# Turning x1 for the gated feed-forward network: from DMA blocks and a VectorE transpose to TensorE transposes

## The reference, cut to what matters

```python
x = L0_attn_x                                        # (2, 2048, 256)
x = layernorm(x + (h + m))                           # h = x + mamba2(rmsnorm(x)),  m = relu(rmsnorm(h) @ w_fc)**2 @ w_proj
def ffn(x):                                          # hidden width 1024, four layers of scaled ternary weights
    h = silu(tlin(x, w1, s1)) * tlin(x, w2, s2)      # 256 -> 1024, twice
    h = gelu(tlin(h, h1, sh1))                       # 1024 -> 1024
    h = gelu(tlin(h, h2, sh2))                       # 1024 -> 1024
    return tlin(h, w3, s3)                           # 1024 -> 256
out = layernorm(x + ffn(x))
```

## Time and profile before

| | |
|---|---|
| median of 3 runs | 1225.31 us (1225.02 to 1226.35) |
| the profiled execution | 1225.02 us |
| its span, first to last instruction | 1223.3 us |
| mean granted clock of TensorE | 0.997 of 2.4 GHz |
| busy: TensorE, VectorE, ScalarE, GpSimd | 98%, 64%, 53%, 19% of the span |

### The profile page before, as it was taken

How to read it: one execution, slowest core, us unless ns; L and a number is a source line. 1 busy time by engine, 2 the same in 40 slices (tenths; PEclk the granted TensorE clock), 3 DMA queues, 4 the chain that set the end, 5 groups by cost and what they waited for, 6 DMA issues and landing times.

```text
span 1223.3 us, 19219 instructions
## 1 busy us (share of the span) xinstructions
PE 1196.2 (98%) x6468; PEld 1007.0 (82%) x6468; DVE 783.2 (64%) x1363; ACT 646.0 (53%) x1213; POOL 232.8 (19%) x210
## 2 busy tenths in 40 slices
PE   8899999999999999999999999999999999999996
PEld 6678888888888888788888888888888888888885
DVE  6898898989899898855535336345363363543633
ACT  6788888878788888666224124142141331422420
POOL 0517153534434261610000000000000000000000
PEclk9999999999999999999999999999999999999998
DMA  7222211222322221134500202002002020020000
GB/s 268 97 82 75 83 68 51 63 88 75 97 75 97 75 73 64 66 128 182 201 1 1 52 1 51 0 0 51 0 6 45 0 51 0 0 51 0 18 1 18
DMA packets 60696, 72.05 MB, mean 59 GB/s; under 512 B 33520, under 2 KB 52080, under 8 KB 58736
## 3 DMA queue, kind: packets, MB, share of 16 engines
q1 hardware_dynamic: 60656, 71.51, 18.0%
HBM read 63.10 MB, written 22.03 MB: 70 GB/s over the span
## 4 chain that ended last, share of the span: by engine, by line
issue 53%; POOL 0%; DVE 0%; POOLq 0%; DVEq 0%
POOL rsv_b L1882 0%; DVE o_sb L1959 0%; POOLq L1880 0%; DVEq L1712 0%; POOL rsv L235 0%; POOLq L441 0%
## 5 line engine op out<-in xcount | busy, mean ns | idle before, releaser
L1866 ACT ACTIVATE full<-bank,scale 128x512 f32<-128x512 f32 x128 | 88.3, 690 | 383.0 <-PE bank L1774 383.0
L1774 PE MATMUL bank<-hB_hi,h_sb 128*128 128x512 f32 x512 | 199.6, 390 | 0.0
L1774 PE MATMUL bank<-hB_lo,h_sb 128*128 128x512 f32 x512 | 199.5, 390 | 0.0
L1774 PE MATMUL bank<-hA_hi,h_sb 128*128 128x512 f32 x512 | 199.3, 389 | 0.0
L1774 PE MATMUL bank<-hA_lo,h_sb 128*128 128x512 f32 x512 | 199.2, 389 | 0.0
L1928 DVE CAST hA_hi<-full 128x512 fp32r<-128x512 f32 x64 | 27.3, 427 | 173.1 <-ACT full L1866 173.1
L1882 POOL TENSOR_TENSOR rsv_b<-mv_b,eps 128x4 f32<-128x4 f32 x8 | 10.7, 1341 | 618.2 <-DVE mv_b L187 618.2
L1774 PEld LDWEIGHTS bank<-hA_hi,h_sb 128*128 128x128 f32 x512 | 96.1, 188 | 20.1
L1774 PEld LDWEIGHTS bank<-hA_lo,h_sb 128*128 128x128 f32 x512 | 96.1, 188 | 20.0
L1774 PEld LDWEIGHTS bank<-hB_hi,h_sb 128*128 128x128 f32 x512 | 96.3, 188 | 19.2
L1774 PEld LDWEIGHTS bank<-hB_lo,h_sb 128*128 128x128 f32 x512 | 96.3, 188 | 19.0
(11 more groups left out here) (230 smaller groups left out, 2981.5 us busy)
## 6 DMA issues: line engine op xcount, KB each, us to landing
chk_xh<-w_ffn SPq DMA_DIRECT2D x16, 704.0 KB, 4.2
ffn_raw<-w_ffn SPq DMA_DIRECT2D x8, 1408.0 KB, 6.7
h_sb<-ffn_raw SPq DMA_DIRECT2D x2, 4096.0 KB, 19.5
xT<-x_t SPq DMA_DIRECT2D x8, 512.0 KB, 6.2
x_res<-x SPq DMA_DIRECT2D x8, 512.0 KB, 3.8
x_rows<-x SPq DMA_DIRECT2D x8, 512.0 KB, 3.3
x_in<-x_rows SPq DMA_DIRECT2D x8, 512.0 KB, 4.9
x_in<-x SPq DMA_DIRECT2D x7, 512.0 KB, 4.9
```

Of the source, the lines that this page charges most:

```text
L1774: ins = pe.matmul(o, a_, b_, start=first and n == 0, stop=last and n == 1, skip_group_check=True)
L1866: nc.scalar.activation(full[:, n % FULL, :], b[:], ACT.Gelu, scale=scale[:, 1 + n // KH, n % KH:n % KH + 1]).then_inc(s_gd, 1)
```

## The change

Seven of the eight tiles were turned by DMA and VectorE. All are now turned as the first one was. `load_blocks`, its semaphore and the VectorE transpose are gone; in layer 2, ahead of channel 6, TensorE runs `turn(pe, i + 1)`; ScalarE and VectorE call `turned_hi` and `turned_lo`, which read PSUM where they read SBUF before. One number in a wait of VectorE (L1898) follows, since `s_ti` now counts ten a tile. The load of `x_in` is as it was.

```diff
@@ -1673,10 +1673,6 @@
         w3_sb = sb("w3_sb", [P, KH, D], F32R)
         s3_b = sb("s3_b", [P, D])
         x1_in, x1_res = x_in, sb("x1_res", [P, CH, D])
-        SQ = 32
-        BLOCK_LOADS = 16 * KD * (P // SQ)
-        x1_blocks = x1[:].rearrange("p c n -> p (c n)").rearrange("p (k n) -> p k n", k=KD)
-        x1T = chk_xh[:, PART:].rearrange("p (k n) -> p k n", k=KD)
         hA_hi, hA_lo = sb("hA_hi", [P, KH, TILE], F32R), sb("hA_lo", [P, KH, TILE], F32R)
         hB_hi, hB_lo = sb("hB_hi", [P, KH, TILE], F32R), sb("hB_lo", [P, KH, TILE], F32R)
         FULL = 3
@@ -1695,8 +1691,6 @@
         s_h2 = sem("h2_loaded")
         s_w3 = sem("w3_loaded")
         s_kept = sem("x1_kept")
-        s_blocks = sem("x1_blocks_loaded")
-        s_turned = sem("x1_blocks_turned")
         s_gi = sem("ffn_act_item_ready")
         s_shi = sem("hidden_hi_ready")
         s_ghi = sem("gated_hi_ready")
@@ -1715,15 +1709,6 @@
                 def load(at):
                     sp.dma_start(x1_in[:], rows(x1_dram, at)).then_inc(s_x1i, 16)

-                def load_blocks(at):
-
-                    flat = x1_dram.rearrange("n f -> (n f)")[bass.ds(at, TILE * D)]
-                    src = flat.rearrange("(m b k j a) -> j b k m a", b=SQ, k=KD, j=P // SQ, a=SQ)
-                    for j in range(P // SQ):
-                        for k in range(KD):
-                            dst = x1_blocks[j * SQ:(j + 1) * SQ, k, :].rearrange("b (m a) -> b m a", a=SQ)
-                            sp.dma_start(dst, src[j][:, k, :, :]).then_inc(s_blocks, 16)
-
                 def store(i, at):
                     sp.wait_ge(s_o, CH * i + CH)
                     sp.dma_start(rows(out, at), o_sb[:]).then_inc(s_store, 16)
@@ -1738,14 +1723,11 @@
                 sp.wait_ge(s_td, KD + B_DVE_BANKS)
                 sp.wait_ge(s_x1o, 16 * TILES + 1)
                 load(TILE * D)
-                load_blocks(TILE * D)
                 with sp.Fori(0, TILES - 2) as i:
                     at, at_next = sp.snap(i * (TILE * D)), sp.snap((i + 2) * (TILE * D))
                     store(i, at)
                     sp.wait_ge(s_kept, i + 2)
                     load(at_next)
-                    sp.wait_ge(s_turned, i + 1)
-                    load_blocks(at_next)
                 store(TILES - 2, (TILES - 2) * TILE * D)
                 i = TILES - 1
                 for n in range(2):
@@ -1811,6 +1793,8 @@
                         pe.wait_ge(s_h2, 16)
                         pe.wait_ge(s_w3, 16)
                     for j in range(KH):
+                        if more and j == TURN:
+                            turn(pe, i + 1)
                         channel(2, h2_sb, hB_hi, hB_lo, j)
                         if j >= BEHIND:
                             out_rows(j - BEHIND)
@@ -1866,9 +1850,7 @@
                         nc.scalar.activation(full[:, n % FULL, :], b[:], ACT.Gelu,
                                              scale=scale[:, 1 + n // KH, n % KH:n % KH + 1]).then_inc(s_gd, 1)
                         if more and n == 2 * KH + TURN - 1:
-                            act.wait_ge(s_turned, i + 1)
-                            for k in range(KD):
-                                nc.scalar.activation(x1T_hi[:, k, :], x1T[:, k, :], ACT.Copy).then_inc(s_thi, 1)
+                            turned_hi(act, i + 1)

                 with act.Fori(0, TILES - 1) as i:
                     tile(i, True)
@@ -1895,7 +1877,7 @@
                         nc.vector.tensor_tensor(lo, full[:, n % FULL, :], hi.bitcast(F32), ALU.subtract).then_inc(s_split, 1)

                     def gated(j):
-                        dve.wait_ge(s_ti, KH * i + KD + j + 1)
+                        dve.wait_ge(s_ti, NBD * i + KD + j + 1)
                         dve.wait_ge(s_gd, NBA * i + j + 1 + B_ACT_BANKS)
                         if j >= FULL:
                             dve.wait_ge(s_split, 3 * KH * i + j - FULL + 1)
@@ -1928,15 +1910,8 @@
                         nc.vector.tensor_copy(hi[:, n % KH, :], full[:, n % FULL, :]).then_inc(s_shi, 1)
                         dve.wait_ge(s_shi, 2 * KH * i + n - KH + 1)
                         lo(n, hi[:, n % KH, :], lo_[:, n % KH, :])
-                        if more and n == 2 * KH + TURN - 2:
-                            dve.wait_ge(s_blocks, BLOCK_LOADS * (i + 1))
-                            nc.vector.transpose(x1T.rearrange("p k n -> p (k n)"),
-                                                x1_blocks.rearrange("p k n -> p (k n)")).then_inc(s_turned, 1)
                         if more and n == 2 * KH + TURN - 1:
-                            for k in range(KD):
-                                dve.wait_ge(s_thi, KD * (i + 1) + k + 1)
-                                nc.vector.tensor_tensor(x1T_lo[:, k, :], x1T[:, k, :], x1T_hi[:, k, :].bitcast(F32),
-                                                        ALU.subtract).then_inc(s_td, 1)
+                            turned_lo(dve, i + 1)

                 def finish_last(i):

```

## The result

| | before | after |
|---|---|---|
| median of five runs | 1225.38 us | 1232.18 us (1231.77 to 1233.21) |
| ratio | | 1.0052, 95% interval 1.0041 to 1.0064 |
| span of the profiled execution | 1223.3 us | 1228.8 us |
| first matmul of the second part, in the profile | 567.87 us | 567.21 us |
| a tile of the second part, first matmul to first matmul | 80.71 us | 81.59 us |

The kernel is 0.5% slower. The windows of the kernel after answer to those of the earlier trace rows: tile 1, then tiles 6 and 7 as far as channel 7 of layer 2 (length, busy time and count of each engine, clock, DMA share, GB/s).

A forecast was written before the change was run, and what follows sets the result against it. TensorE, without a gap in the second part, was taken as the bound: 7 x 0.96 = 6.7 us added, nothing given back, so 1232.0 us on the median, 0.55% slower; range 1230.2 to 1234.0 us.

The forecast's parts named there:

- What bounds: Second part: TensorE runs matmuls without a gap, busy for all 80.71 us of a tile; anything added costs its whole time.
- What is removed costs nothing: Per turn, seven times: eight small DMAs, one VectorE transpose and SBUF reads go, worth 0 on the path.
- The comparison of tile 6 with tile 7: Same matmuls up to channel 7 of layer 2, with and without turning work: 73.22 against 73.23 us.
- What is added: Eight TensorE transposes per turn, tiles 0 to 6: 0.96 us a turn, 6.7 us in all, on the path.
- the lower bound: Price of a turn from the first part's eight transposes of h, without a load to wait for: 0.87 us.
- The waits in the loop: Rival: register and wait instructions show in six loop turns, 1.12 us each; 7.7 us in all, 1233.0 us; chance 0.12.
- One after another: Rival: a turn's eight transposes do not overlap, 2.18 us per turn, 16.1 us in all, 1241.4 us; chance 0.02.
- clock: Rival: TensorE falls to 1.2 GHz for the transposes and the channel behind; 39 us in all, 1264 us; chance 0.02.
- ScalarE's copies 0.7 us behind the first transpose: At each turn, ScalarE's copies from PSUM were to start near 0.7 us after the first transpose starts.

The follow-up runs named there:

- experiments 1 and 2: 1: kernel before without block loads and VectorE transpose, nothing in their place, 1226.04 us (0.9998); 2: changed kernel with both put back, result unused, 1232.12 us (1.0048).
- experiment 9: Kernel before with the first tile also turned by blocks, its VectorE transpose, ScalarE copies and VectorE subtractions placed late in the first part: 1223.94 us, ratio 0.9984.
- experiment 7: The changed kernel measured once more, unchanged: 1232.26 us, ratio 1.0048 to the kernel before.

## Why the prediction was right

- *What bounds.* TensorE without a gap in the second part: so it was, in every profile; the tile's length answered only to what was put into TensorE's queue.
- *What is removed costs nothing.* The comparison of tile 6 with tile 7 held; experiments 1 and 2 confirm it from both sides (80.71 and 81.59 us, to the last digit).
- *What is added.* The mechanism was right, its size 9% too high: 0.96 us a turn was read from `turn(pe, 0)`, and 0.88 was measured. As the price of that one call the reading was good, since taking it away gave 0.98 us (experiment 9). But 0.03 us ahead of its transposes and 0.04 us inside them are in no turn of the loop. The 0.03 is a wait for the load of `x_in`, which the trace of before has as well, too short for its list of waits:

```profile
L540 SPq DMA_DIRECT2D x_in<-x_rows x1: 379/379/379, 541.7 to 541.7; - x1
DMA to landing us min/median/max: 7.9/7.9/7.9
```

Issued at 541.68 us and landed 7.9 us later, the load is there at 549.53 (unrounded), and the transposes start at 549.58. In all nine profiles with this call its first transpose starts 0.04 to 0.07 us behind that landing. The 0.04 inside goes with it: in experiment 7, where the load was clearly late, the eight took 0.84 us as here (552.01 to 552.85), and in the loop, where it has long landed, 0.79 to 0.80. Why a load that has just landed lengthens the group was not looked into. I took the price from a place with a wait in it; the lower bound, from the transposes of h (0.87), which wait for no load, was the better witness.
- *The median came out closer than the reasoning.* 7 x 0.96 = 6.7 met a difference of medians of 6.8, but 6.2 us is what the tiles show, the ratio of that same comparison (1.0052) says 6.4, and the later ratios (1.0048, 1.0048, 1.0046 for the same eight transposes a turn) say 5.6 to 5.9. That 1232.0 was met within 0.2 us has some luck in it.
- *The waits in the loop.* The register and wait instructions cost nothing: the turn of tile 0, with constants, and those of the loop all take 0.79 to 0.80 us from first start to the next matmul.
- *One after another, clock.* Eight took 1.04 us, not 2.2, and the granted clock was 1.00 through eight and sixteen transposes. The Trainium skill ("TensorE: Matmul & The Clock Gate", Part 4: PE-mode transpose) gives about 275 ns for a transpose in a kernel's context; the trace agrees as to the duration (273 ns), and shows that the path pays 109 ns of it. As for transposes not counting as work for the clock gate, no run here shows a fall of the clock by them.
- *ScalarE's copies 0.7 us behind the first transpose.* 0.64 us, and nobody waited for the result.

## What to carry to other kernels

When one engine runs without a gap, compare a stretch that has some other work beside it with the same stretch that has not; equal lengths mean that moving that work onto the full engine can only lose. Price an instruction by what it adds between the starts of its neighbours, not by its duration, and take it from several places, since a single place may hide a wait. Work that is free on another engine is free only in the right place of that engine's order: with VectorE's transpose ahead of the layer norm's sums and ScalarE's copies, which wait for it, ahead of m, the way to the second part took 1.70 us longer than with both behind. When an engine comes late, look whether it was busy or itself waiting before that.

## What the runs showed of the hardware that was not expected

- A TensorE instruction of 128 columns costs 0.109 us between starts, whether it is a float32 transpose or a float32r matmul, with 128 or (transposes) 64 columns of weights, and one of 64 columns 0.11, while 256 columns cost 0.12 and 512 cost 0.227 us. From 512 to 256 the step falls by 0.107 us, from 256 to 128 by 0.011. What sets this floor was not found. All these instructions load weights from 128 partitions, and no run varied that.
- A narrow instruction's price appears partly behind it: a lone transpose is followed after 0.03 us by the next matmul, and after another 0.32 instead of 0.23 us by the one behind.
- The granted clock can fall in the first 40 us of an execution (0.57 of full speed as a mean from 16 to 20 us, 0.74 from 34 to 40 us) or not fall at all, with the same code; with both falls, all that follows came 2.1 us later.
